# A hybrid attention and feed-forward block on one core: a double-buffered first stage, sums in smaller matmuls, an order by part, and one scaling moved from GpSimd to ScalarE

## The chip, the core and the metric

The kernel runs on one NeuronCore of one Trainium2 chip. The metric is the device time of one execution in microseconds (us). A core has five instruction streams that run side by side and meet only at semaphores: PE (TensorE, with its weight loads, PEld), DVE (VectorE), ACT (ScalarE), POOL (GpSimd) and SP (SyncE, which issues all DMAs here). Each stream executes in the order in which it is written, so an instruction that waits holds back all that stands behind it on its own engine.

## The reference, cut to what matters

The input is x of shape (4, 1024, 256): B = 4 sequences of L = 1024 rows. All is float32. Two blocks follow each other, each with a residual:

```python
def layernorm(x): return (x - mean(x)) / sqrt(var(x) + 1e-5)

h = layernorm(x)                                    # (4, 1024, 256), 4 heads of 64
q, k, v = silu(short_conv4(h @ W.T)) for Wq, Wk, Wv # causal, 4 taps per channel
beta = sigmoid(h @ Wb.T)                            # one per row and head
q, k = q * rsqrt(sum(q*q) + 1e-6), k * rsqrt(sum(k*k) + 1e-6)
# delta rule, per head, in chunks of 32 rows:
T = inverse(I + strictly_lower(beta * k @ k.T));  u = T @ (beta * v);  w = T @ (beta * k)
for chunk: u_adj = u - w @ S;  o = q @ S + lower(q @ k.T) @ u_adj;  S = S + k.T @ u_adj
local_s, local_m, local_l = depthwise causal FIR of v with 3, 15 and 63 taps
p = softmax((h @ gate_w + gate_b) / exp(log_temp)) * (1 - 5 eps) + eps   # 5 per head
o = p0*local_s + p1*local_m + p2*local_l + p3*delta + p4*v
x = x + layernorm(rmsnorm(o) @ Wo.T)

h = layernorm(x); hp = h shifted by one row
r = sigmoid(mix(h, hp, mu_r) @ Wr.T);  ka = relu(mix(h, hp, mu_k) @ Wk.T) ** 2
x = x + layernorm(r * (ka @ Wv.T))
```

## The kernel before, in words

The kernel cuts each sequence into 16 chunks of 64 rows and has five parts in time. Every engine has its own program, a list of small functions in an order written out by hand.

**First stage** (functions `a_...`, per sequence b = 0 to 3, `def sequence(b)` on each engine). DVE takes the statistics of 8 row tiles (L788, L792, L795), POOL the power -0.5 (L418), DVE normalizes (L802), PE transposes (L1142), ACT copies to `xnT` (L575), PE projects to v (L1152, four quarters q), ACT starts the convolution (L581), DVE adds its three other taps (L813), ACT applies silu (L587), PE transposes windows of v (L1163), and ACT copies each of them twice over, to `vwin` (L592) and to `vb` (L601, in two halves of 64 partitions), which SP stores in `v_scratch` (L272). The gates are 16 small matmuls of 24 columns per sequence (L1170), copied by DVE (L824). The input `xa`, the transposed rows `xnT` and the values `vb` have one buffer each: `a_xT_out` of a sequence waits for the matmuls and the stores of the one ahead of it, and `a_silu` for its last windows (`a_win`).

**FIR stage.** 64 tiles: matmuls against Toeplitz matrices that SP loads in 8 groups (`load(g)`, L255, L256), the gates' product on DVE (L892), two sums on POOL (L430, L432), transposes (L1222), and a copy to `fir`.

**Lead.** Chunks m = 0 to 7 are projected, convolved and silu'd to k and q (PE `proj` L1272, ACT `tap` L658, DVE `conv` L915, ACT `silu` L667), squared (L673) and summed (PE `sumsq` L1282, DVE `sumsq_out` L921, PE `sums_twice` L1288, DVE `norms_in` L931), and multiplied to grams (PE `gram` L1307, DVE `at_parts` L939, ACT `gram_out` L682). k and q share the PSUM banks 0 and 1 with those sums. SP stores a gram of each chunk and, after four chunks, loads them as blocks (`blocks_in`, L338). POOL then solves the group of four chunks, column after column, for 31 columns (`solve_column`, L499, L501). SP stores the solution (`solved_store`, L342) and loads it for each chunk (`solved_in`, L356, L361).

**Chunk steps n = 0 to 7** do chunk n of the scan and of all that follows, and the lead's work of chunk n + 8; groups 1 and 2 are solved meanwhile by POOL. **Steps n = 8 to 15**, the tail, have no lead work; group 3 is solved in the first of them. In each step run: the state's part (`scan_k` L1339, `rest_in` L975, `scan_u` L1348, `u_out` L697, `scan_o`), the mixed output (`o_scaled` L981, `o_summed` L987, `o_meansq` L991, L993, a power on POOL, `o_normed` L998), its projection (`o_turn` L1380, `y_rows`), three normalizations (`row_stats` L1005, L1009, L1012, a power on POOL (L510), `row_norm` L1017), and the feed-forward part (`shifted`, `mix` L1055, `ffn_k`, `ffn_r`, `ffn_v`, `ffn_out` L1064). POOL also makes the norms (L450, L453), scales the values by the keys' norm (`values`, L461), adds gated values and FIR parts (`direct`, L469, L472) and the last residual (`output`, L522). SP loads the values of chunk n (`values_in`, L304, L305) after `values` and `direct` of chunk n - 1.

All engines walk one table, `for n in range(-9, 19): chunk_step(n)`, in which lead, chunk and tail share one order.

## Time and profile before

| | |
|---|---|
| median of 3 runs | 829.26 us (817.76 to 842.99) |
| the profiled execution | 832.73 us, of which 830.9 us are the span |
| first stage, until the FIR stage's first matmul | 155.1 us |
| FIR stage, until the last transposes | 87.9 us |
| lead, until chunk 0's `rest_in` | 142.4 us |
| steps between `rest_in` of chunks 0 and 8 | 226.6 us |
| steps between `rest_in` of chunks 8 and 15 | 172.3 us |
| from `rest_in` of chunk 15 to the end | 46.7 us |

The times of the parts are cut at the start of an instruction of the trace: the first L1213 at 155.1, L975 of chunks 0, 4, 8, 12 and 15 at 385.4, 496.2, 612.0, 720.7 and 784.3 us. No engine is busy throughout: PE has 620.2 us of matmuls in the span (75%), DVE 494.2 (59%), POOL 424.8 (51%) and ACT 272.3 (33%).

### The profile page before, as it was taken

The page shows a single profiled execution, that of the slowest core. Times are in us where ns is not written, and L with a number is a line of the kernel's source. Part 1 is how long each engine was busy: PE and PEld are TensorE (multiplying, and loading weights), DVE is VectorE, ACT ScalarE, POOL GpSimd, SP SyncE. Part 2 cuts the span into 40 slices and gives each one's busy share as a digit, 9 for nine tenths or more (in the row PEclk, how much of TensorE's full clock was granted, in tenths as well). Part 3 has the DMA queues.
Part 4 walks back from the last instruction along what each step waited for, and adds up shares of the span by engine and source line. Part 5 has one row for each costly group of instructions (what it writes and reads, how often), then busy time and mean ns, then how long its engine had stood idle before and what let it go on. Part 6 is the DMA issues. An engine that isn't in the chain of part 4 may idle for free.

```text
span 830.9 us, 19290 instructions
## 1 busy us (share of the span) xinstructions
PE 620.2 (75%) x7556; PEld 496.5 (60%) x7556; DVE 494.2 (59%) x1194; ACT 272.3 (33%) x603; POOL 424.8 (51%) x513
## 2 busy tenths in 40 slices
PE   1866857488887774868878998988968576777854
PEld 1655646354555562657767886776767565666642
DVE  2556355343434433454688887878966575777762
ACT  1656564410114321333333344324412121222221
POOL 6000000155550000884889856998649998555521
PEclk9878777698988766698999998999998899999996
DMA  8723521288821114114212143321232020322101
GB/s 264 213 52 102 150 54 51 51 228 229 227 60 27 27 27 51 27 39 106 55 28 63 50 102 52 76 49 38 77 77 47 14 49 31 92 46 49 28 20 25
DMA packets 102634, 63.38 MB, mean 76 GB/s; under 512 B 81041, under 2 KB 95249, under 8 KB 100881
## 3 DMA queue, kind: packets, MB, share of 16 engines
q1 hardware_dynamic: 102544, 62.16, 29.2%
q8 instruction: 60, 0.98, 0.5%
q14 instruction: 30, 0.24, 0.1%
HBM read 43.19 MB, written 18.95 MB: 75 GB/s over the span
## 4 chain that ended last, share of the span: by engine, by line
POOL 39%; issue 13%; PE 7%; DVE 4%; SPq 3%; DMA 2%; ACT 1%; POOLq 0%; DVEq 0%; ACTq 0%
POOL seq L501 10%; POOL seq L499 8%; POOL arena L510 6%; POOL arena L450 4%; POOL arena L472 3%; PE bank L1272 3%; POOL arena L469 2%; SPq L338 2%; POOL arena L522 2%; POOL arena L461 2%; DVE arena L915 2%; PE bank L1282 1%; DMA seq<-gram_scratch 1%; PE bank L1307 1%; SPq L317 1%
## 5 line engine op out<-in xcount | busy, mean ns | idle before, releaser
L915 DVE SCALAR_TENSOR_TENSOR arena<-bank,small,arena 128x256 f32<-128x256 f32 x192 | 91.9, 482 | 40.6 <-ACT arena L658 35.9
L510 POOL TENSOR_TENSOR arena<-arena,neg_half 128x2 f32<-128x2 f32 (+1 forms) x64 | 64.3, 1005 | 91.0 <-DVE arena L1012 66.6
L501 POOL TENSOR_TENSOR seq<-seq 128x31 f32<-128x31 f32 (+15 forms) x124 | 85.4, 688 | 9.7
L499 POOL TENSOR_TENSOR seq<-seq 128x31 f32<-128x31 f32 (+15 forms) x124 | 70.2, 566 | 7.8
L1213 PE MATMUL bank<-arena 128*64 128x192 f32 x512 | 61.3, 367 | 11.5 <-DMA arena<-fms 7.1
L813 DVE SCALAR_TENSOR_TENSOR cva<-bank,small,cva 128x256 f32<-128x256 f32 x96 | 39.8, 477 | 50.3 <-ACT cva L581 50.1
L430 POOL TENSOR_TENSOR seq<-seq 128x256 f32<-128x256 f32 x32 | 23.3, 728 | 83.8 <-DVE seq L892 56.5
L892 DVE TENSOR_TENSOR seq<-bank,seq 128x384 f32<-128x384 f32 x64 | 35.3, 557 | 51.8 <-PE bank L1213 41.0
L658 ACT ACTIVATE arena<-bank,small 128x256 f32<-128x256 f32 x64 | 30.4, 475 | 75.5 <-PE bank L1272 75.5
L1152 PE MATMUL bank<-seq,w_v 128*128 128x259 f32 x128 | 45.2, 513 | 12.2 <-DVE cva L813 10.2
L1307 PE MATMUL bank<-arena 64*64 64x128 f32 x512 | 40.4, 303 | 17.8 <-issue 17.8
L418 POOL TENSOR_TENSOR rs_a<-ve_a,neg_half 128x8 f32<-128x8 f32 x4 | 6.6, 1642 | 92.1 <-DVE ve_a L795 92.1
L1272 PE MATMUL bank<-arena,w_k 128*128 128x268 f32 x128 | 46.3, 509 | 4.7 <-DVE seq L931 4.7
L1412 PE MATMUL bank<-seq,w_fk 128*128 128x256 f32 x128 | 34.9, 419 | 19.2 <-DVE seq L1055 19.2
L1213 PEld LDWEIGHTS bank<-arena 128*64 128x64 f32 x512 | 34.5, 148 | 23.5 <-DMA arena<-fms 7.7
L1272 PE MATMUL bank<-arena,w_q 128*128 128x268 f32 x128 | 36.7, 414 | 14.3 <-DVE arena L915 14.3
L481 POOL MEMSET seq<- 128x1024 f32 x4 | 3.8, 952 | 85.0 <-DVE seq L954 85.0
L450 POOL TENSOR_TENSOR arena<-seq,powers 128x16 f32<-128x16 f32 x16 | 46.4, 2902 | 0.3 <-POOL seq L501 0.3
L1307 PEld LDWEIGHTS bank<-arena 64*64 64x64 f32 x512 | 32.4, 151 | 21.3 <-issue 20.6
L1282 PEld LDWEIGHTS bank<-cst,arena 128*64 128x64 f32 x512 | 36.9, 158 | 12.3 <-issue 12.3
L1282 PE MATMUL bank<-cst,arena 128*64 128x32 f32 x512 | 38.4, 239 | 7.8 <-ACT arena L673 7.8
L1152 PEld LDWEIGHTS bank<-seq,w_v 128*128 128x128 f32 x128 | 31.5, 258 | 21.3 <-ACT seq L575 8.9
(137 smaller groups left out, 1499.6 us busy)
## 6 DMA issues: line engine op xcount, KB each, us to landing
arena<-fms SPq DMA_DIRECT2D x8, 1280.0 KB, 10.7
arena<-fl SPq DMA_DIRECT2D x8, 1024.0 KB, 5.3
arena<-xnT_scratch SPq DMA_DIRECT2D x32, 134.0 KB, 2.6
xnT_scratch<-seq SPq DMA_DIRECT2D x4, 1027.0 KB, 6.1
seq<-x SPq DMA_DIRECT2D x4, 1024.0 KB, 7.7
v_scratch<-seq SPq DMA_DIRECT2D x8, 512.0 KB, 5.3
arena<-v_scratch SPq DMA_DIRECT2D x16, 256.0 KB, 2.7
arena<-x SPq DMA_DIRECT2D x64, 64.0 KB, 2.3
```

What stands on the lines that cost most here:

```text
L450: pool.tensor_tensor(rk, ssel[:, slot_of(n)], powers[:, :, :], ALU.pow).then_inc(s["norms"], 1)
L499: pool.tensor_tensor(part, below, above, ALU.mult).then_inc(s["solve"], 1)
L501: last = pool.tensor_tensor(into, into, part, ALU.add)
L510: pool.tensor_tensor(dst, src, half8 if k == U else neg_half[:, 0:k], ALU.pow).then_inc(s[dst_sem], 1)
L813: nc.vector.scalar_tensor_tensor(cva[:, i, :], bank[2 + i][:, j:j + 256], conv_w[:, 2, i, j:j + 1], cva[:, i, :], ALU.mult, ALU.add).then_ ...
L892: nc.vector.tensor_tensor(fprod[:, q % (2 * FPAIRS), :], bank[q % 4][:, 0:2 * ROW], fgate[:, q // (TILES // 2), :], ALU.mult).then_inc(s[" ...
L915: nc.vector.scalar_tensor_tensor(cv[:, t], ps[:, :, j:j + C], conv_w[:, 1 - t // 2, t % 2, j:j + 1], cv[:, t], ALU.mult, ALU.add).then_inc ...
L1152: last = mm(bank[2 + oh][:, 0:PAD + 256], w["v"][:, kh, P * oh:P * oh + P], xnT[:, kh, 256 * q:256 * q + 256 + PAD], start=(kh == 0), stop ...
L1213: last = mm(out_[HH[i], :, 64 * hh:64 * hh + C], vwin[:, P * pr + 64 * hh + d, :], toep[:, g % 2, :, cin, :], start=True, stop=True)
L1272: last = mm(bank[g][:, 0:B * (C + PAD)], w["kq"[kind]][:, kh, P * g:P * g + P], xwin4[:, m % 2, kh], start=(kh == 0), stop=(kh == 1))
L1282: last = mm(bank[1][0:C, 32 * a:32 * a + 32], sq[:, a], headsel, start=True, stop=True)
L1307: last = mm(bank[2][q, P * u:P * u + P], kq5[q, slot_of(m), G4 * g + u, 0, :], kq5[q, slot_of(m), G4 * g + u], start=True, stop=True)
```

## The change

- **First stage.** `xa`, `xnT` and `vb` get a second set, carved from `fir`, which is free then. A sequence's input comes in two halves, each with its own semaphore. Statistics, powers and normalization go by halves and quarters. The small inputs and the v weights have semaphores of their own and stand ahead of the other weights. All engines' work of sequence b + 1 stands among that of sequence b.
- **Copies of v.** The values are stored with 128 columns of a pair of heads in a row; the two copies of 64 partitions per window become one of 128.
- **Gates.** 16 matmuls with the rows as weights become 8 with `w_gate` (padded to 32 columns) as weights and 256 rows moving, written to four groups of 32 PSUM partitions, then a copy on ACT and two transposes.
- **Sums of squares.** 16 matmuls (128 rows, 64 columns, 32 moving), a DVE step, one matmul and two DVE copies become 32 matmuls of 64 by 64 with 4 moving columns, k apart from q, and one DVE step.
- **FIR.** Its transposes come in pairs.
- **Order by part.** Every step is `lead_step(n)`, `chunk_step(n)`, `tail_step(n)` with an order of its own, and other offsets between the engines.
- **Keys' scale.** `values` moves from one POOL instruction to eight on ACT, one for each unit (sequence and pair).

```diff
-        xa = carve(seq, sa, M_TILES, D)
+        sx = [0]
+        xa2 = [carve(seq, sa, M_TILES, D), carve(fir_flat, sx, M_TILES, D)]
...
-        xnT = carve(seq, sa, HALVES, LP)
+        xnT2 = [carve(seq, sa, HALVES, LP), carve(fir_flat, sx, HALVES, LP)]
...
-        vb = carve(seq, sa, N, PAIRS, DK)
+        vb2 = [carve(seq, sa, N // 2, PAIRS, P), carve(fir_flat, sx, N // 2, PAIRS, P)]
...
             def values_in(n):
                 sp.wait_ge(s["vp"], n)
                 sp.wait_ge(s["ov"], 2 * n)
-                sp.dma_start(v_c, v_dram[n]).then_inc(s["v_in"], 16)
+                for hh in range(2):
+                    sp.dma_start(v_c[HH[hh]], v_dram[n][:, :, :, HH[hh]].rearrange("t r b d -> t (r b) d")).then_inc(s["v_in"], 16)
...
+            def values(n):
+                act.wait_ge(s["v_in"], 32 * n + 32)
+                act.wait_ge(s["norms"], 2 * n + 1)
+                act.wait_ge(s["rest"], n)
+                for u in range(U):
+                    last = act.activation(vp[:, u, :], v_c[:, u, :], ACT.Copy, scale=rk[:, 0, u:u + 1])
+                last.then_inc(s["vp"], 1)
...
-                if q == 0:
-                    act.wait_ge(s["a_proj"], b * 8)
-                    act.wait_ge(s["a_gate"], b * 1)
-                    act.wait_ge(s["a_xT_stored"], b * 16)
+                if q == 0 and b >= 2:
+                    act.wait_ge(s["a_proj"], (b - 1) * 8)
+                    act.wait_ge(s["a_gate"], b - 1)
+                    act.wait_ge(s["xT_odd_stored" if b % 2 else "xT_even_stored"], 16 * (b // 2))
...
-                for m in range(M_TILES):
-                    for kh in range(HALVES):
-                        last = mm(bank[6][:, H * NG * m:H * NG * (m + 1)], xnT[:, kh, PAD + P * m:PAD + P * m + P],
-                                  w_gate[:, kh, :], start=(kh == 0), stop=(kh == 1))
+                for kh in range(HALVES):
+                    for j in range(4):
+                        last = mm(bank[6][32 * j:32 * j + 32, 0:2 * P], w_gate[:, kh, :],
+                                  xnT2[b % 2][:, kh, PAD + 256 * j:PAD + 256 * j + 256], start=(kh == 0), stop=(kh == 1))
...
-                for a in range(2 * U):
-                    last = mm(bank[1][0:C, 32 * a:32 * a + 32], sq[:, a], headsel, start=True, stop=True)
-                last.then_inc(s["sumsq"], 1)
+                for u in range(U):
+                    for q in HH:
+                        last = mm(bank[1][q, NONE * (U * kind + u):NONE * (U * kind + u) + NONE], sq[q, U * kind + u], ones[q],
+                                  start=True, stop=True)
+                last.then_inc(s["sumsq_" + "kq"[kind]], 1)
...
-            for n in range(-9, 19):
+            for n in range(-10, 20):
+                lead_step(n)
                 chunk_step(n)
+                tail_step(n)
```

The order moves on all engines. Three places are shown: DVE in the first stage, SP where a group's solution is stored, and POOL in a step in which it solves.

DVE, first stage, in the middle of a sequence. L788 is the statistics, L792 and L795 their end, L802 the normalization, L813 the convolution (6 for a quarter), L824 the gates. Before:

```order
L813 SCALAR_TENSOR_TENSOR cva<-bank,small,cva 128x256 x18
L788 BN_STATS stats_a<-seq 128x6 x8
L792 BN_AGGR mv_a<-stats_a 128x2 x8
L795 TENSOR_SCALAR ve_a<-mv_a 128x8
L824 COPY gates<-bank 64x6x8 x8
L813 SCALAR_TENSOR_TENSOR cva<-bank,small,cva 128x256 x6
L802 TENSOR_SCALAR seq<-seq,mv_a,rs_a 128x256 x8
```

The change (L997 is the convolution, L985 the normalization, L1009 the gates, L970 the statistics):

```order
L970 BN_STATS stats_a<-fir 128x6 x4
L974 BN_AGGR mv_a<-stats_a 128x2 x4
L977 TENSOR_SCALAR ve_a<-mv_a 128x4
L997 SCALAR_TENSOR_TENSOR cva<-bank,small,cva 128x256 x6
L985 TENSOR_SCALAR seq<-fir,mv_a,rs_a 128x256 x2
L1009 COPY gates<-bank 64x6x8 x8
L997 SCALAR_TENSOR_TENSOR cva<-bank,small,cva 128x256 x6
L985 TENSOR_SCALAR seq<-fir,mv_a,rs_a 128x256 x6
```

The last normalization of a sequence stood at the sequence's end; it now stands two quarters earlier and in pieces between convolutions of the sequence ahead, so that its transposes can start while that one still runs.

SP, where the solution of group 1 is stored (`solved_scratch<-seq`). `arena<-v_scratch` is the load of a chunk's values, `arena<-xnT_scratch` of a window. Before:

```order
L323 DMA gram_scratch<-arena 128x512 [waits g_tok_1,g_tok_0]
L342 DMA solved_scratch<-seq 128x1024 [waits solved]
L305 DMA arena<-v_scratch 128x512 [waits ov,vp]
L317 DMA out<-arena 64x256 [waits y_out]
L317 DMA out<-arena 64x256 x3
L356 DMA seq<-gram_scratch 32x8x32 [waits off_a,turned,y_stored]
L361 DMA seq<-solved_scratch 32x8x32 x2
```

The change:

```order
L356 DMA solved_scratch<-seq 128x1024 [waits solved]
L370 DMA seq<-gram_scratch 32x8x32 [waits off_a,turned,y_stored]
L375 DMA seq<-solved_scratch 32x8x32 x2
L370 DMA seq<-gram_scratch 32x8x32
L375 DMA seq<-solved_scratch 32x8x32 x2
L312 DMA arena<-xnT_scratch 128x4x67 [waits proj_q0,proj_q1,proj_k1,proj_k0]
L312 DMA arena<-xnT_scratch 128x4x67
L319 DMA arena<-v_scratch 64x8x64 [waits ov,vp]
```

The load of the values stood right behind the store of the solution; it now also has the six loads of the solution (which wait until the store has landed) and two of a window ahead of it.

POOL, around the norms of chunk 2, while group 1 is solved (L499 and L501, in the change L536 and L538, are a column's product and sum; the powers of 128x8 belong to `o_normed`, those of 128x2 to the three normalizations). Before:

```order
L510 TENSOR_TENSOR arena<-arena,neg_half 128x2 [waits st2]
L450 TENSOR_TENSOR arena<-seq,powers 128x16 [waits vp,norms,ssel]
L453 TENSOR_TENSOR arena<-gates,arena 128x8 [waits o1,norms]
L461 TENSOR_TENSOR arena<-arena 128x512 [waits rest,norms,v_in]
L499 TENSOR_TENSOR seq<-seq 128x11x21 [waits solve]
L501 TENSOR_TENSOR seq<-seq 128x11x21 [waits solve]
L499 TENSOR_TENSOR seq<-seq 128x12x20 [waits solve]
L501 TENSOR_TENSOR seq<-seq 128x12x20 [waits solve]
L499 TENSOR_TENSOR seq<-seq 128x13x19 [waits solve]
L501 TENSOR_TENSOR seq<-seq 128x13x19 [waits solve]
L510 TENSOR_TENSOR arena<-arena,neg_half 128x8 [waits oms]
L469 TENSOR_TENSOR arena<-arena,gates 128x512 [waits o2,v_in]
```

The change:

```order
L547 TENSOR_TENSOR arena<-arena,neg_half 128x8 [waits oms]
L553 COPY arena<-arena 128x8 [waits xf,mix_r,mix_k]
L495 TENSOR_TENSOR arena<-seq,powers 128x16 [waits vp,norms,ssel]
L498 TENSOR_TENSOR arena<-gates,arena 128x8 [waits o1,norms]
L506 TENSOR_TENSOR arena<-arena,gates 128x512 [waits o2,v_in]
L509 TENSOR_TENSOR arena<-arena,fir 128x512 [waits ov]
L547 TENSOR_TENSOR arena<-arena,neg_half 128x2 [waits st1]
L536 TENSOR_TENSOR seq<-seq 128x11x21 [waits solve]
```

The scaling (L461) is gone from POOL, and no column is left between the norms and `direct` (L506, L509): the columns of a step now all stand between the power that waits for `st1` and the one that waits for `oms`.

## Rows read from the trace of the kernel before

**Rows 1.** Busy time by engine in nine stretches (us from the span's start).
```profile
core 0: us, PE busy (x) PEld busy (x) DVE busy (x) ACT busy (x) POOL busy (x), PEclk, DMA share, GB/s
20.00:155.10 135.10, 92.33 (x442) 76.13 (x440) 72.17 (x226) 81.72 (x180) 4.92 (x3) 0.76 0.32 96
155.10:243.00 87.90, 76.03 (x603) 45.42 (x604) 35.32 (x64) 10.26 (x19) 46.53 (x64) 0.90 0.65 179
249.00:315.00 66.00, 50.37 (x329) 38.59 (x327) 28.52 (x68) 23.07 (x57) 0.00 (x0) 0.73 0.10 26
496.20:612.00 115.80, 103.10 (x1631) 86.72 (x1630) 94.42 (x220) 43.15 (x100) 90.12 (x109) 0.97 0.27 62
612.00:720.70 108.70, 74.89 (x1302) 64.79 (x1302) 68.22 (x152) 23.03 (x44) 90.45 (x109) 0.89 0.21 48
720.70:784.30 63.60, 50.24 (x980) 43.37 (x980) 47.46 (x112) 17.27 (x33) 38.02 (x34) 1.00 0.20 45
```
**Rows 2.** Groups by line, first stage: busy us, mean ns, idle before, releaser.
```profile
L813 DVE SCALAR_TENSOR_TENSOR cva<-bank,small,cva 128x256 f32<-128x256 f32 x96 | 39.8, 477 | 50.3 <-ACT cva L581 50.1
L601 ACT ACTIVATE seq<-bank 64x256 f32<-64x256 f32 x64 | 24.4, 381 | 1.6
L1170 PE MATMUL bank<-w_gate,seq 128*128 128x24 f32 x128 | 18.0, 297 | 0.0
L788 DVE BATCH_NORM_STATS2 stats_a<-seq 128x6 f32<-128x256 f32 x32 | 10.9, 414 | 17.0 <-DMA small<-smalls 11.9 <-DMA seq<-x 5.1
```
**Rows 3.** Timeline: projection quarters 0 and 1 of sequence 0.
```profile
20.10 2.92 PE L1152 MATMUL bank<-seq,w_v 128*128 128x259 f32 x8
25.38 1.99 PE L1152 MATMUL bank<-seq,w_v 128*128 128x259 f32 x8 [1.92 <-DVE cva L813]
```
**Rows 4.** Timeline of the FIR stage: 8 matmuls.
```profile
159.43 1.48 PE L1213 MATMUL bank<-arena 128*64 128x192 f32 x16
```
**Rows 5.** Timeline of the lead: chunks 2 and 3.
```profile
281.07 3.88 PE L1272 MATMUL bank<-arena,w_k 128*128 128x268 f32 x8 [0.67 <-DVE seq L931]
291.47 3.47 PE L1282 MATMUL bank<-cst,arena 128*64 128x32 f32 x32 [0.91 <-ACT arena L673]
294.87 1.97 PE L1307 MATMUL bank<-arena 64*64 64x128 f32 x16
298.07 3.91 PE L1272 MATMUL bank<-arena,w_k 128*128 128x268 f32 x8 [0.67 <-DVE seq L931]
```
**Rows 6.** Timeline: store and load of group 0's solution, next values.
```profile
374.60 0.33 SPq L342 DMA_DIRECT2D solved_scratch<-seq  x1
377.22 0.66 SPq L356 DMA_DIRECT2D seq<-gram_scratch  x1
383.10 0.38 SPq L305 DMA_DIRECT2D arena<-v_scratch  x1
```
**Rows 7.** Groups by line, chunk steps.
```profile
L461 POOL TENSOR_TENSOR arena<-arena 128x512 f32<-128x512 f32 x16 | 18.1, 1132 | 0.0
L1282 PE MATMUL bank<-cst,arena 128*64 128x32 f32 x512 | 38.4, 239 | 7.8 <-ACT arena L673 7.8
L1329 PE MATMUL bank<-seq 32*32 32x32 f32 x512 | 11.5, 195 | 0.0
L645 ACT ACTIVATE seq<-bank 64x128 f32<-64x128 f32 x2 | 0.4, 264 | 6.0 <-PE bank L1237 6.0
```
**Rows 8.** DMA issues: KB each, us to landing.
```profile
arena<-v_scratch SPq DMA_DIRECT2D x16, 256.0 KB, 2.7
```
**Rows 9.** Windows with L501 alone: its busy time in two solves.
```profile
331.00:374.60 43.60, 20.80 (x31) 0.83 0.12 32
496.20:612.00 115.80, 21.52 (x31) 0.97 0.27 62
```
**Rows 10.** Timeline: `o_summed` beside a busy POOL and beside a quieter one.
```profile
568.41 1.48 DVE L987 TENSOR_TENSOR arena<-arena 128x512 f32<-128x512 f32 x1
748.03 0.69 DVE L987 TENSOR_TENSOR arena<-arena 128x512 f32<-128x512 f32 x1
```

869 lines of the change are left out of this document (577 added, 292 removed).

## The prediction

> **What bounds the kernel now.** The first view is the table of stretches [rows 1], because the change touches parts with different limits. From 20 to 155.1 us, the first stage, no engine is full: PE is busy for 92.3 of 135.1 us, ACT for 81.7, DVE for 72.2. In the groups by line [rows 2] DVE's convolution waits 50.1 us for ACT's first tap, and nothing but one quarter of one sequence is under way: a latency bound. In the FIR stage PE is busy for 76.0 of 87.9 us. The lead (249 to 315) is a chain too, with PE busy for 50.4 of 66 us. From 496.2 to 612.0, four chunk steps, PE is busy for 103.1 of 115.8 us, DVE for 94.4, POOL for 90.1: near a bound of three engines. In the tail POOL is full while it solves a group (90.5 of 108.7), and after that (720.7 to 784.3, three steps of 21.2) nobody is: PE 50.2, DVE 47.5, POOL 38.0 of 63.6 us.
>
> **The first stage.** Work per sequence, from [rows 1, 2]. DVE: 72.2/4 = 18.0 us. ACT: 81.7/4 = 20.4, less half of L601 (24.4/2/4 = 3.1), plus one copy of a gate bank (0.4) = 17.7. PE: 92.3/4 = 23.1 at a mean granted clock of 0.76, less the gates' 18.0/4 = 4.5, plus the new gates. Those are 8 matmuls over 256 columns. Four matmuls of the projection over 259 columns take 1.99 us [rows 3], so one after another the new gates take 4.0. In the FIR stage 8 matmuls of 192 columns, alternating between two groups of 64 columns, take 1.48 us [rows 4], 0.96 ns per column against 1.92, so two groups run side by side. I take that factor of two, 2.0 us, and 0.3 for the two transposes: PE 20.9.
> The Trainium skill, "TensorEngine Tiling (Array Packing)", section Key Properties, lets different tiles run in parallel; with four tiles it would be 1.0 us and the stage 4 us shorter in all. The same section says that a change of the tiling mode drains the engine, which speaks against gates of 32 columns between matmuls of 128; no row shows a gap of a size that matters.
> Now a sequence takes (155.1 - 20.1)/4 = 33.8 us. With two sets of buffers b + 1 can fill the waits of b, and the limit is PE's 20.9. Three engines in a fixed order with quarter steps don't fit without loss: I take 22.5. The ends: 18.0 (DVE's sum, PE at a better clock) and 28 (half of the waits stay). Start: DVE's first statistics wait until 11.9 for the small inputs, the last of the first DMAs [rows 2]; half a sequence ahead of the weights frees about 7.5 us, so that quarter 1 of sequence 0 is projected at 20 rather than 27.4 [rows 3]. Then 3 x 22.5 = 67.5, and for the rest of the last sequence 20.5 (three quarters of a sequence and 4 us of the softmax's start, which now stands ahead of the last convolution). FIR starts at 108, against 155.1: **-47** (-61 to -27). The values' stores move 512 instead of 256 bytes in a piece; what waits for them at the stage's end waits as before.
> **FIR stage.** Same loads, same products, transposes in pairs: 0 (-3 to +3).
>
> **The lead.** One chunk takes 298.07 - 281.07 = 17.0 us [rows 5]. The chain: projections of k at 281.07 until the last square of q, which frees L1282 at 291.47 (10.4, unchanged), sums 3.47, second gram 1.97, one more matmul and DVE's two copies until 298.07. In the change the k sums run earlier, and of the q sums there are 16 small matmuls. The nearest row is L1329, 16 matmuls in 32x32 at 11.5/16 = 0.7 us [rows 7]; the other end is half of the old sums, 1.7. I take 1.0. The gram follows, and DVE's one step runs beside it. 10.4 + 0.3 (the square of the other half is now last) + 1.0 + 1.6 (the gram at a mixed clock) = 13.3. Four chunks: 4 x 3.7 = 14.8, less 1.4 because the fourth gram is read out after, no longer ahead of, the next projection, and 1 because the first chunk was shorter: **-12** (-16 to -5). The solve of group 0 and the transfers around it stay: they wait for that gram.
>
> **Steps 0 to 7.** PE loses per step 38.4/16 = 2.4 plus 0.4 and gains 1.4 for the sums: about 1.4 less, 24.4. DVE 23.3, POOL per step without the scaling (1.13 [rows 7]) 21.4 on average, but unevenly: a solve is 62 instructions, 39 us, plus a gap of 0.08 after each, 44 us in three steps, the middle one the heaviest (columns of 256 elements). Beside it POOL has 11.5 us a step. So the three steps cost POOL 12, 17, 11.5 of columns + 11.5 + 1.5 of waits for DVE = 25, 30, 24.5; in the lighter two DVE (23.3 + 2.5 of waits for powers) sets 26. The fourth is PE's or DVE's, 25.2. That is 107.2 for a group, against 115.8.
> A new wait takes part of it back. SP now has the load of chunk 4's values behind the solution's store, six loads and two more. From store to the same place took 383.10 - 374.60 = 8.5 us, and the values take 2.7 more [rows 6, 8], 11.2 in all. POOL's last column ends 3.6 us ahead of step 3's start (0.3, the wait for `o_meansq`, 1.9 for the power, and idle time), so the values land at 7.6, while `direct` wants them at 3.5. POOL loses 4.1, of which 2.8 reach DVE's `residual` by way of `f_normed`. So 110 for a group. Steps 4 to 7: 110 against 115.8. Steps 0 to 3: 26 + 30 + 26 + 28, against 110.8 with a first step of 24.9: no gain. **-5** (-16, when the wait is hidden, to +6).
> ACT's eight scalings replace one instruction of 1.13 us. Nearest is L645, 0.26 us for 128 columns [rows 7]: 2.1 us for the eight, beside other work, as ACT is busy for 43 of 115.8 us.
>
> **The tail.** Steps 8 to 10 are POOL's: 25, 30, 24.5, step 11 about 20.5, together 100, against 108.7; I take -6. Steps 12 to 15, walked in the new order: DVE's 15.8 us, plus its waits for three powers (3), for `direct`, which now stands behind the second power (0.8), and for PE and ACT ahead of `shifted` (0.6) = 20.2, against 21.2: -3. After chunk 15 `ffn_out` of older chunks is out of the way: -2. **-11** (-18 to +4).
>
> **Sum.** -47 - 12 - 5 - 11 = -75: 832.7 - 75 = 757.7 for a profiled execution. The one shown lies 0.4% above the median of the runs, so 755 on the median's scale.
>
> **Rivals.**
> *A, the orders fit better.* The transfers hide and steps 0 to 7 come to PE's 25.2 on average: 8 x (28.3 - 25.2) = 25, 20 more than above: 735. For it speaks that such an order is possible by the sums; against it the middle third on POOL.
> *B, the first stage stays a chain.* With a period of 28 FIR starts at 20 + 84 + 24 = 128: 775. For it: the clock of 0.76, at which PE alone needs 21, and three engines that hand each other pieces of half a microsecond.
> *C, POOL and DVE hold each other up.* `o_summed` took 1.48 us beside POOL's scaling and 0.69 elsewhere [rows 10], while L501's 31 sums took 20.8 us beside an idle DVE and 21.5 beside a full one [rows 9], so that POOL hardly suffers. If in a denser step the columns slow down by 10% and DVE's five two-input steps by a third, 9 solve steps get 2 us each: 773. The Trainium skill, "GPSIMD Engine Reference", Specifications, says that the SBUF interfaces are shared with VectorE and contended by instructions with two SBUF inputs; by this rule it is C.
> *D, slower.* SP's queue gates every step: `values_in` waits for ACT's scaling and POOL's `direct` with the output, gram and x transfers queued behind it, and if each of 14 further steps waits as long as the whole chain of 6.5 us beyond the need, 14 x 6.5 = 91: 846, which is where 2% slower begins. Against it: SP's list for a step is about 15 us of issues in 26.
> *E, no gain that counts:* B and half of D together, 816 to 848.
>
> **Numbers.** Forecast 0.55, A 0.12, B 0.17, C 0.10, D 0.03, E 0.03. Two per cent is about what a measurement of this kernel tells from no change (its own runs lie within 1.6% of the median), so below 813 is faster. Faster 0.94, same 0.03, slower 0.03. The range takes in A, B and C with the first stage's own ends: 733 to 790.
>
> **What would show it.** The first FIR matmul at 108 (100 to 118), with PE over 85% busy between 25 and 100. The k projections of the lead 13.3 apart. The load of values at SP's head 8 us after the second solution's store, POOL idle for about 4 us ahead of chunk 4's `direct`, and steps of 26, 30, 26 and 28 us. L461's successor on ACT at 0.2 to 0.3 us each. Tail steps of 20.2. It is wrong if the first stage ends after 125, or if the steps that solve stay at 30.

## The result, and the profile after

The changed kernel takes 786.2 us in the median of four runs (785.3 to 789.75), against 826.15 us for the kernel before (817.76 to 842.99, four runs of the same comparison). The ratio is 0.956, with a 95% interval of 0.947 to 0.965. The forecast was 755 us with a range of 733 to 790: the sign held, and the range did with 4 us to spare, but the gain in the profiled spans is 47.4 us (830.9 to 783.5), where 75 were forecast. Cut at the same instructions as before (the first FIR matmul, the lead's first projection, `rest_in` of chunks 0, 4, 8, 12 and 15):

| part | before | after | change | forecast |
|---|---|---|---|---|
| first stage | 155.2 | 114.2 | -41.0 | -47 |
| FIR stage | 93.7 | 89.8 | -3.9 | 0 |
| lead | 136.5 | 125.8 | -10.7 | -12 |
| steps 0 to 3 | 110.8 | 113.6 | +2.8 | 0 |
| steps 4 to 7 | 115.8 | 118.7 | +2.9 | -5.8 |
| steps 8 to 11 | 108.7 | 108.2 | -0.5 | -6 |
| steps 12 to 14 | 63.6 | 68.8 | +5.2 | -3 |
| end | 46.6 | 44.5 | -2.1 | -2 |

Of the 27.6 us that are missing, 24 lie in the steps and the end, 6 in the first stage and 1 in the lead; the FIR stage gave back 4. Each part is one trace, and how far a part moves by itself can be read from the runs below. In the changed kernel and the nine of them that leave both parts' programs as they are (e1 to e8 and x3, apart from a few loads), the FIR stage takes 85.0 to 94.0 us and the lead 119.4 to 128.5. So the 3.9 us of the FIR stage are within that spread, and the 10.7 of the lead are not. The busy times of the changed kernel by stretch, in the columns of [rows 1]:

```profile
20.00:114.20 94.20, 58.33 (x370) 45.48 (x370) 67.76 (x213) 62.83 (x148) 5.03 (x5) 0.86 0.52 151
443.36:562.07 118.71, 104.48 (x1784) 88.32 (x1783) 96.41 (x222) 50.69 (x133) 86.56 (x105) 0.96 0.29 62
562.07:670.23 108.16, 76.94 (x1281) 65.68 (x1282) 63.46 (x141) 29.29 (x75) 80.68 (x100) 0.79 0.21 46
670.23:739.00 68.77, 58.24 (x973) 48.78 (x973) 48.09 (x113) 22.57 (x57) 33.42 (x30) 0.88 0.21 46
```

POOL's work fell in steps 8 to 11 from 90.5 to 80.7 us (4.9 of that are the four scalings, most of the rest is work that now falls outside the stretch), yet they take as long. In the last stretch the granted clock fell from 1.00 to 0.88, and PE's busy time rose from 50.2 to 58.2 us; DVE's is nearly the same (47.5 and 48.1).

**First stage.** From the timeline, PE's first quarters of sequences 1 and 2 with DVE's wait; the window from 31 to 52 us in the columns of [rows 1]; SP's issues; then the group by line of DVE's convolution, and transfers of the window from 36 to 75 us with their time to landing:

```profile
33.83 1.99 PE L1396 MATMUL bank<-fir,w_v 128*128 128x259 f32 x8 [1.11 <-DVE cva L997]
51.48 1.99 PE L1396 MATMUL bank<-seq,w_v 128*128 128x259 f32 x8 [1.11 <-DVE cva L997]
70.94 1.41 DVE L970 BATCH_NORM_STATS2 stats_a<-fir 128x6 f32<-128x256 f32 x4 [19.22 <-DMA fir<-x]
```
```profile
31.00:52.00 21.00, 17.00 (x115) 13.64 (x115) 20.35 (x66) 18.02 (x45) 2.01 (x2) 1.00 0.53 142
```
```profile
42.51 1.13 SPq L270 DMA_DIRECT2D arena<-fl  x1
43.68 1.12 SPq L271 DMA_DIRECT2D arena<-fms  x1
...
47.55 1.41 SPq L254 DMA_DIRECT2D fir<-x  x2
```
```profile
L997 DVE SCALAR_TENSOR_TENSOR cva<-bank,small,cva 128x256 f32<-128x256 f32 x96 | 40.1, 478 | 7.3 <-ACT cva L653 7.0
```
```profile
arena<-fms SPq DMA_DIRECT2D x2, 1280.0 KB, 18.0
...
fir<-x SPq DMA_DIRECT2D x2, 512.0 KB, 23.7
```

The same quarter of the next sequence comes 17.6 us later (51.48 - 33.83), a pace well below the 22.5 of the forecast: DVE no longer waits 50 us for the first tap [rows 2] but 7. Then DVE stands for 19.2 us. The rows of the last sequence are asked for at 47.55 behind the FIR stage's first taps, four transfers of 4.6 MB together, and a store of 1 MB, and take 23.7 us to land. The forecast's sum of a slower pace and no such wait came out near the truth for the wrong reason. The Trainium skill, "DMA: Bandwidth & Descriptors", section on queues, rings and completion order, says that descriptors of a ring are consumed in order; the trace fits this, since the same pair of transfers for the sequence ahead, asked for at 22.2 with no taps in front, landed in 7.5 us by the same view. It doesn't tell the order in the ring from plain sharing, as the DMA engines were busy throughout (a share of 1.01 from 48 to 55 us, at 231 GB/s).

**The lead.** The projections of k stand 12.2 us apart, where 17.0 was before [rows 5] and 13.3 forecast. Timeline, the projections of k of two chunks:

```profile
216.07 3.21 PE L1540 MATMUL bank<-arena,w_k 128*128 128x268 f32 x8
...
228.23 3.56 PE L1540 MATMUL bank<-arena,w_k 128*128 128x268 f32 x8
```

**Step 3**, where group 1's solution is handed over. The timeline, with the store (L356), the normed output (L1188), the load of chunk 4's values (L319), the solved blocks' first product (L1583), the turn of the output (L1645) and POOL's direct part (L506):

```profile
424.40 0.34 SPq L356 DMA_DIRECT2D solved_scratch<-seq  x1
426.19 0.69 DVE L1188 TENSOR_TENSOR arena<-arena 128x512 f32<-128x512 f32 x1 [0.53 <-POOL arena L547]
431.73 1.23 SPq L319 DMA_DIRECT2D arena<-v_scratch  x2
432.00 1.06 PE L1583 MATMUL bank<-seq 32*32 32x32 f32 x32 [4.74 <-DMA seq<-solved_scratch]
432.99 1.97 PE L1645 MATMUL bank<-cst,arena 64*64 64x64 f32 x32
435.41 1.06 POOL L506 TENSOR_TENSOR arena<-arena,gates 128x512 f32<-128x512 f32 x1 [5.50 <-DMA arena<-v_scratch]
```

The predicted wait is there: the load of the values comes 7.3 us behind the store (8.5 in the forecast), and POOL stands for 5.5 us. A second one was not predicted. PE has the solved blocks' product ahead of `o_turn` (L1645), so the output, normed at 426.9, is turned only at 433.

**The tail**, step 13. POOL's direct part (L506, L509), DVE's `x_normed` (L1207), the next load of values, PE's first solved product and `y_rows` (L1652):

```profile
698.68 1.06 POOL L506 TENSOR_TENSOR arena<-arena,gates 128x512 f32<-128x512 f32 x1
698.74 2.73 DVE L1207 TENSOR_SCALAR arena<-seq,arena 128x256 f32<-128x256 f32 x2 [0.81 <-POOL arena L547]
699.81 1.51 POOL L509 TENSOR_TENSOR arena<-arena,fir 128x512 f32<-128x512 f32 x1
701.40 1.23 SPq L319 DMA_DIRECT2D arena<-v_scratch  x2
707.69 0.71 DVE L1150 STREAM_TRANSPOSE seq<-seq 128x512 f32<-128x512 f32 x1 [1.48 <-DMA seq<-solved_scratch]
711.21 3.78 PE L1652 MATMUL bank<-w_o,arena 128*128 128x256 f32 x8
```

And the groups by line for two of the three forms of L1207 (x from SBUF, y from PSUM) and for ACT's values:

```profile
L1207 DVE TENSOR_SCALAR arena<-seq,arena 128x256 f32<-128x256 f32 x32 | 30.3, 988 | 16.0 <-POOL arena L547 16.0
L1207 DVE TENSOR_SCALAR arena<-bank,arena 128x256 f32<-128x256 f32 x32 | 15.9, 539 | 11.2 <-POOL arena L547 11.1
L841 ACT ACTIVATE arena<-arena 128x64 f32<-128x64 f32 x128 | 32.2, 336 | 7.8 <-POOL arena L495 3.9 <-DMA arena<-v_scratch 3.9
```

Two instructions of `x_normed` take 2.73 us beside the direct part, and 0.73 in the last chunk's step, which has none; the mean of one was 408 ns before and is 988 now. `y_rows` takes 3.78 us here and 1.99 in step 11: from 710 to 716 us the granted clock is 0.50. SP's next loads, of values and behind them of solved blocks, wait for the same direct part and land late: DVE waits 1.48 us here and 6.2 in the three steps.

### The profile page after: what moved, and what is told of

It reads as the page before. It is cut to its first block, busy times and chain, and to the rows that moved or that the text cites. A ratio compares the mean times of both kernels' runs of the same rounds, so it can differ in the third digit from the quotient of the medians.

```text
span 783.5 us, 20240 instructions
## 1 busy us (share of the span) xinstructions
PE 592.6 (76%) x7980; PEld 477.9 (61%) x7980; DVE 492.6 (63%) x1166; ACT 284.2 (36%) x703; POOL 407.5 (52%) x502
## 4 chain that ended last, share of the span: by engine, by line
POOL 30%; PE 14%; issue 10%; DVE 8%; SPq 7%; DMA 3%; ACT 1%; POOLq 0%; DVEq 0%; ACTq 0%
POOL seq L538 10%; POOL seq L536 9%; POOL arena L547 4%; PE bank L1652 4%; PE bank L1540 2%; POOL arena L509 2%; POOL arena L495 2%; DVE arena L1112 2%; SPq L352 2%; SPq L375 2%; PE bank L1572 2%; PE bank L1551 1%; POOL arena L506 1%; PE bank L1645 1%; DMA seq<-gram_scratch 1%
## 5 line engine op out<-in xcount | busy, mean ns | idle before, releaser
L547 POOL TENSOR_TENSOR arena<-arena,neg_half 128x2 f32<-128x2 f32 (+1 forms) x64 | 61.9, 966 | 110.4 <-DVE arena L1202 74.4
L1112 DVE SCALAR_TENSOR_TENSOR arena<-bank,small,arena 128x256 f32<-128x256 f32 x192 | 91.7, 482 | 38.2 <-ACT arena L775 33.6
L538 POOL TENSOR_TENSOR seq<-seq 128x31 f32<-128x31 f32 (+15 forms) x124 | 86.7, 699 | 9.7
L536 POOL TENSOR_TENSOR seq<-seq 128x31 f32<-128x31 f32 (+15 forms) x124 | 71.6, 577 | 8.3
L1479 PE MATMUL bank<-arena 128*64 128x192 f32 x512 | 57.0, 372 | 13.2 <-DMA arena<-fms 10.7
L1479 PEld LDWEIGHTS bank<-arena 128*64 128x64 f32 x512 | 38.5, 155 | 25.5 <-DMA arena<-fms 11.4
L1572 PEld LDWEIGHTS bank<-arena 64*64 64x64 f32 x512 | 34.1, 157 | 27.3 <-issue 26.9
L495 POOL TENSOR_TENSOR arena<-seq,powers 128x16 f32<-128x16 f32 x16 | 49.6, 3101 | 0.3 <-POOL seq L538 0.3
L997 DVE SCALAR_TENSOR_TENSOR cva<-bank,small,cva 128x256 f32<-128x256 f32 x96 | 40.1, 478 | 7.3 <-ACT cva L653 7.0
L1540 PE MATMUL bank<-arena,w_q 128*128 128x268 f32 x128 | 36.0, 404 | 10.7 <-DVE arena L1112 10.7
L775 ACT ACTIVATE arena<-bank,small 128x256 f32<-128x256 f32 x64 | 29.4, 471 | 40.5 <-PE bank L1540 40.5
L1652 PE MATMUL bank<-w_r,seq 128*128 128x256 f32 x128 | 35.1, 421 | 9.6 <-DVE seq L1245 9.6
L784 ACT ACTIVATE arena<-arena 128x256 f32<-128x256 f32 x64 | 25.7, 413 | 40.6 <-DVE arena L1112 40.3
L1207 DVE TENSOR_SCALAR arena<-seq,arena 128x256 f32<-128x256 f32 x32 | 30.3, 988 | 16.0 <-POOL arena L547 16.0
L1652 PE MATMUL bank<-w_o,arena 128*128 128x256 f32 x128 | 38.1, 449 | 1.4 <-ACT arena L827 1.4
L462 POOL TENSOR_TENSOR rs_a<-ve_a,neg_half 128x4 f32<-128x4 f32 x8 | 8.2, 1028 | 58.8 <-DVE ve_a L977 58.6
## 6 DMA issues: line engine op xcount, KB each, us to landing
arena<-fms SPq DMA_DIRECT2D x8, 1280.0 KB, 12.2
```

The lines of the kernel that those rows point to most:

```text
L495: pool.tensor_tensor(rk, ssel[:, slot_of(n)], powers[:, :, :], ALU.pow).then_inc(s["norms"], 1)
L536: pool.tensor_tensor(part, below, above, ALU.mult).then_inc(s["solve"], 1)
L538: last = pool.tensor_tensor(into, into, part, ALU.add)
L547: pool.tensor_tensor(dst, src, half8 if k == U else neg_half[:, 0:k], ALU.pow).then_inc(s[dst_sem], 1)
L997: nc.vector.scalar_tensor_tensor(cva[:, i, :], bank[2 + i][:, j:j + 256], conv_w[:, 2, i, j:j + 1], cva[:, i, :], ALU.mult, ALU.add).then_ ...
L1112: nc.vector.scalar_tensor_tensor(cv[:, t], ps[:, :, j:j + C], conv_w[:, 1 - t // 2, t % 2, j:j + 1], cv[:, t], ALU.mult, ALU.add).then_inc ...
```

## Experiments

Times are medians of four runs or more, ratios are to the kernel before on the same chip (0.956 for the changed kernel). As these medians move by 1% between executions, what one stretch takes is read from the traces, from `rest_in` to `rest_in`. That is one trace for each kernel, and two kernels with the same steps 0 to 7 (e3 and e7) differ there by 1.8 us in sum.

### Steps 3 and 7: one wait, the other, and both

The values first, on SP (e1):
```diff
+ if 1 <= n + 4 < 9: values_in(n + 4)
  if 0 <= n + 2 < 8 and solving(n + 2)[1] == 2: solved_store(...)
  ...
- if 1 <= n + 4 < 9: values_in(n + 4)
```


> Of steps 0 to 7, on SP's queue, the load of a chunk's values is moved ahead of the wait for the solved group (the changed kernel has it behind: at 431.73 us, after the store at 424.40). Theory V (the values' load behind the solved store is what makes steps 3 and 7 long): the load of chunk 4 is issued before 424, POOL's direct no longer waits 5.5 us for it and runs at about 430, step 3 (30.0) and the two steps at group 2 (34.1 and 29.4) lose 3 to 5 us each time: 775 to 780 against 786. Theory T (the solved blocks' own load, for which TensorE's order stands 4.7 us until 432.0, is the bound): TensorE starts off_first at 432.0 all the same, nothing or at most 1 us per group is gained: 784 to 787.

The solved blocks later on three engines in steps 3 and 7 (e2):
```diff
  PE : - off_first(n + 1); o_turn(n); gram(n + 8, 0); y_rows(n); off_second(n + 1); gram(n + 8, 1)
       + o_turn(n); gram(n + 8, 0); y_rows(n); off_first(n + 1); gram(n + 8, 1); off_second(n + 1)
  ACT: off_out(n + 1) behind oT_out(n) and gram_out
  DVE: solved_turn(n + 1), at_parts(n + 8, 1) and residual(n) behind y_stats(n), ahead of off_in(n + 1)
```


> In steps 3 and 7 alone, TensorE does off_first of the next chunk behind y_rows and not ahead of o_turn; ACT's off_out goes behind oT_out and VectorE's block transpose behind the statistics of y, so that the normed output, its turn and the product with the output weights no longer stand behind the load of the solved blocks. SP's order is the changed kernel's. Theory T: the output turn starts at about 427 in place of 433, so 4 us go at step 3 and as many at step 7: 777 to 780. Theory V: chunk 4's values still land at 435, POOL's direct and ACT's scaled values with them, and the residual of the next chunk waits for these: 784 to 787.

Both (e3 = e1 + e2):

> Both edits together: values' load ahead of the solved store, and TensorE, ACT and VectorE past the solved blocks in steps 3 and 7. If the two waits stand side by side and either alone keeps the step long (each of the single edits gives little), this gives 8 to 11 us: 775 to 778. If one alone is the bound, it equals that one. A rival (C of the prediction, the two engines hold each other up): the stall only gives way to slower vector work and a POOL that is late with the next group's solve, and the gain is under 3 us.

Measured: e1 782.6 us (0.937, 0.927 to 0.946), e2 788.8 us (775 to 790, and one run of 1049 us whose cause is unknown; they scatter too much for a ratio), e3 775.6 us (0.928, 0.920 to 0.935). By the traces step 3 took 30.6 us in the changed kernel, 29.8 in e1, 33.6 in e2 and 28.1 in e3; step 7 took 34.1, 34.2, 37.7 and 30.8. Both single-cause theories fall: in e1 POOL's direct part ran at 428.0 without a wait, but PE still stood 4.6 us; in e2 the output was turned at 426.7, but POOL and ACT stood for the values until 435. The waits stand side by side, and only both edits remove them. Why e2 makes both steps 3 us longer than they were wasn't looked into. The 8 to 11 us expected of e3 came in the median (10.6 under the changed kernel), but not in the steps: from chunk 0 to 15 its trace takes 405.2 us against 409.2. The timeline of e3: the store, the turn, POOL's direct part, the solved product, and then the last gram of the group, read out by ACT (L799), stored (L337) and loaded back (L352):

```profile
418.66 0.34 SPq L356 DMA_DIRECT2D solved_scratch<-seq  x1
421.44 1.15 PE L1652 MATMUL bank<-cst,arena 64*64 64x64 f32 x32
424.13 1.06 POOL L506 TENSOR_TENSOR arena<-arena,gates 128x512 f32<-128x512 f32 x1
426.10 0.69 PE L1590 MATMUL bank<-seq 32*32 32x32 f32 x32
430.39 0.38 ACT L799 ACTIVATE arena<-bank 128x256 f32<-128x256 f32 x1
...
441.37 0.53 SPq L337 DMA_DIRECT2D gram_scratch<-arena  x1
...
445.41 9.11 SPq L352 DMA_DIRECT2D seq<-gram_scratch  x16
```

Yet the four steps from chunk 3's `rest_in` to chunk 7's take 115.2 us in the changed kernel, 115.4 in e1, 114.9 in e4 and 115.2 in e3 (113.2 in e7 below, with the steps of e3, and 120.3 in e2). From the store of group 1's solution until POOL begins on group 2 pass 43.5 us in the changed kernel and 43.5 in e3, and from there to the next store 71.7 in both. Another bound holds there: the last gram of a group is read out at 430.8, waits in SP's queue until 441.4, and comes back by 16 loads, 9.1 us of issues; DVE scales it at 459.0, and POOL, idle for 10.1 us in one piece meanwhile, begins to solve at 462 and has columns until the next handover. The old order was better here. POOL's first instruction of group 2's solve, in the kernel before and in the changed one:

```profile
510.65 0.95 POOL L481 MEMSET seq<- 128x1024 f32 x1
```
```profile
467.87 0.95 POOL L518 MEMSET seq<- 128x1024 f32 x1
```

That is 14.5 us behind chunk 4's `rest_in` before (496.2) and 24.5 in the changed kernel (443.4). For group 3 it is 13.8 and 21.7 us behind chunk 8's.

### The tail: POOL's neighbour

```diff
  def tail_step(n):   # POOL
+     if 9 <= n < N: direct(n)
      if 7 <= n - 3 < N: output(n - 3)
      power(n - 1, "st1", ...); solve_part(n - 1, 2); power(n - 1, "st2", ...)
-     if 9 <= n < N: direct(n)
```


> In the last eight steps POOL does the direct part (L506, L509) of a chunk at the start of its step, ahead of the output add of an earlier chunk, and no longer between the power for x and the norms, where VectorE's x_normed (L1207) ran beside it in 2.73 us for two (0.73 in the kernel before). Theory N (neighbour: POOL's two-input sums slow the vector engine, and the wait for them holds back SP's loads of the values and of the solved blocks): L1207 back to 0.73 for two in these steps, the values' load 7 to 10 us earlier, VectorE's 1.5 to 2.3 us wait for the solved blocks gone: 2.0 + 0.6 to 1.3 us for each of 7 steps, steps 12 to 15 20.2 to 21 us each, 763 to 772 against 786. Rival K (clock): the steps are 22 to 23 long since TensorE's clock is lower than in the kernel before (0.85 against 1.00), the matmul y_rows took 3.78 us for eight where 1.9 is full speed, and that stays: at most 4 us of gain, 782 or more. Rival M (moved): the slowing goes to f_normed and off_in, beside which the direct part now stands, and from them to the statistics of y: half the gain, 775 to 780.

Measured: 769.6 us (0.928, 0.920 to 0.936). Timeline of e4's tail, the direct part and the two SBUF forms of L1207; the window of e4's step 13, in the columns of [rows 1]; then the same step in the changed kernel; then in e1, whose tail has the changed kernel's order, with its `x_normed`:

```profile
709.51 1.06 POOL L506 TENSOR_TENSOR arena<-arena,gates 128x512 f32<-128x512 f32 x1
709.57 2.74 DVE L1207 TENSOR_SCALAR arena<-arena 128x256 f32<-128x256 f32 x2 [0.81 <-POOL arena L547]
...
718.42 0.73 DVE L1207 TENSOR_SCALAR arena<-seq,arena 128x256 f32<-128x256 f32 x2 [0.81 <-POOL arena L547]
```
```profile
694.91:713.74 18.83, 16.90 (x325) 14.40 (x324) 15.97 (x39) 7.40 (x19) 10.97 (x10) 1.00 0.25 54
```
```profile
694.05:716.94 22.89, 19.86 (x325) 16.57 (x326) 16.10 (x38) 7.52 (x19) 11.73 (x11) 0.85 0.21 45
```
```profile
692.80:712.87 20.07, 16.91 (x325) 14.37 (x325) 16.04 (x38) 7.52 (x19) 11.15 (x10) 1.00 0.19 41
697.49 2.74 DVE L1207 TENSOR_SCALAR arena<-seq,arena 128x256 f32<-128x256 f32 x2 [0.81 <-POOL arena L547]
```

The last steps fall from 23.8, 22.9 and 22.0 us to 19.2, 18.8 and 18.8, under the 20.2 of the forecast. `x_normed` is back at 0.73, the slowing moved to `f_normed` (2.74), and DVE's waits for the solved blocks fell from 6.2 us in three steps to 0.4.

But most of the gain is the clock. It is 1.00 again, the level of 2.4 GHz, and `y_rows` takes 1.99. In e1 step 13 ran at 1.00 too, with `x_normed` as slow as in the changed kernel and the same order, and took 20.1 us against 22.9 at 0.85. So of the 4.1 us that this step lost in e4, the clock accounts for 2.8, and the neighbour and the earlier loads together for 1.2. Rival K had the larger cost right; its claim that the low clock stays is false. Without the edit (the changed kernel, e1 to e3, x2 and x3 below) three of eighteen such steps ran at 1.00; with it (e4 to e8) all fifteen did, at 18.8 to 19.8 us. That the shorter waits keep the clock up is argued from this count and not shown: up to 15 us into step 13 the changed kernel and e1 agree within 0.1 us, and then one has the low clock and the other not.

The 769.6 us lie in the range of theory N, but by a sum that it didn't have, since steps 8 to 11 got 10 us longer (118.2 against 108.2). Steps 8 (33.1, 29.5 before the edit) and 11 (28.5, 23.4) became longer: while POOL solves, a direct part ahead of the power for y is on the chain. So it was done from chunk 12 on alone, with both edits of steps 3 and 7 (e7, `if 12 <= n < N: direct(n)` ahead of `output`):

> The kernel with both edits of steps 0 to 7, and the direct part ahead of the output add from chunk 12 on alone; steps 8 to 11 keep the changed kernel's order (in the kernel that moved the direct part everywhere they took 118 us in place of 108). Theory N (neighbour and SP's loads behind the direct part): the three steps 12 to 14 take 18.8 to 19.5 us each in place of 22 to 24, the end 42 to 43: 10 to 13 us under the kernel with both edits, 763 to 767. Rival: step 11 gets what the later steps lose (28.5 in place of 23.4, as it did where the direct part was moved everywhere, since POOL stands for chunk 12's values ahead of the power for y): 768 to 773.

Measured: 765.8 us (0.924, 0.918 to 0.930), step 11 at 23.7, steps 12 to 14 at 18.9, 18.8 and 18.8.

### The loop from the last gram to the solution

The two edits of e3 and three more at once (e5), in part wrong:
```diff
  SP  : + blocks_in(g, first three chunks) one step earlier, behind rows_out;  blocks_in(g, last chunk) in its place
  DVE : blocks_scaled(g) right behind o_normed(n)
  POOL: + norms_power(n + 1) ahead of the power for o;  + 5 columns at the end of steps 0 and 4, in step 8 ahead of norms_q
  POOL: + if 12 <= n < N: direct(n) ahead of output;  SP: values_in(12) ahead of the last solved_store
```


> The two edits of steps 0 to 7 together, and three more. (1) Blocks early: of a group's 16 block loads SP issues the 12 of its first three chunks a step earlier, so that only four stand between the last gram's store and the solve (16 took 9 us of SP's queue, 445.4 to 454.5 us in the kernel with both edits); VectorE scales the blocks right behind o_normed. (2) Solve early: in steps 0, 4 and 8 POOL takes the power for the norms into its idle time ahead of the power for o (it waited 8 to 10 us there) and begins the next group's solve with 5 columns in that step; the columns are shared out anew. (3) Tail: the values of chunk 12 are loaded ahead of the last solved store, and the direct part stands ahead of the output add from chunk 12 on (18.8 us a step there in the kernel with direct moved away). Theory L (steps 4 to 7 take 115.2 us in every kernel so far, since the loop last gram, store, 16 loads, scaling, POOL's 31 columns, solved store, next chunk closes on itself): the loop is shortened by 4 to 7 us, steps 4 to 7 take 105 to 111; with steps 8 to 11 some 3 to 8 shorter and 12 to 15 at 18.8 to 19.5: 745 to 757. Rival P (TensorE is the bound there, busy 101 to 104 of the 115 us): steps 4 to 7 stay at 112 or more, only the tail gains: 760 to 768.

Measured: 774.1 us (0.933, 0.925 to 0.941), no better than e3. Steps 5 and 6 fell to 27.8 and 27.5, but step 4 took 39.1 and step 8 34.0. One row of the waits from 442 to 482 us, for step 4:

```profile
DVE seq L1178 <- DMA seq<-gram_scratch: 7.6, 1, 7.6
```

The last gram still stood behind SP's other work until 454.0, and DVE, which now had the scaling ahead of its other work, stood 7.6 us for it. A wait had been moved onto the chain. So SP's order was written anew (e6), and POOL's columns trimmed (e8):

```diff
  SP, n in (0, 4):
+   gram_store(n+9); rows_in(n+2); values_in(n+4); rows_out(n); rows_in(n+3); gram_store(n+10)
+   solved_store(g); solved_in(n+4); blocks_in(g+1, first three); window_in(n+12); values_in(n+5)
+   gram_store(n+11); blocks_in(g+1, last)
  SP, n == 8: + solved_in(12) right behind solved_store;  POOL: group 3's last columns one place earlier
```


> The trace of the kernel with all five edits showed why its first step of a group took 39.1 us: the last gram of the group was ready at about 431 us but stood in SP's queue until 454, behind output stores and loads, and VectorE stood 7.6 us for the blocks. Here SP's order around steps 0 and 4 is written anew: rows and the third gram ahead of the solved store, then the solved blocks of the next chunk, the 12 early block loads, the values, the last gram and its four loads, and only then the rest; VectorE scales the blocks in the step before (behind the first convolution of the next chunk), POOL begins groups 2 and 3 with 5 and 4 columns ahead of the power for o and gives the last group's solve fewer columns in step 11; in step 8 the solved blocks are asked for right behind the store. The tail has the direct part ahead of the output add from chunk 12 on. Theory L (the loop from the last gram to the solved store bounds steps 4 to 8, and SP's queue order is most of its slack): steps 4 to 7 take 106 to 111 us, steps 8 to 11 96 to 104, steps 12 to 14 18.8 each: 742 to 758. Rival P (TensorE's 101 to 104 busy us and VectorE's 94 of 115, with POOL's 86, leave no room): steps 4 to 7 at 113 or more, total 762 to 772.

```diff
- DVE n in (3, 7): conv(n + 9, 0); blocks_scaled     + n == 3: blocks_scaled; conv(12, 0);  group 3: in step 8
- POOL n == 4: 5 columns ahead of the power for o, 2 behind output;  n == 0: 5
+ POOL n == 4: 5 columns ahead of the power for o;                   n == 0: 3
```


> The kernel with the new SP order around the groups (758.5 us), with POOL's early columns put where they delay nothing: in its trace the 5 columns ahead of the power for o held that power back by 3.1 us and the two behind the output add held the power for y back by 2.9 us, in step 4 (33.7 us), and VectorE's scaling stood behind a convolution that waited for ACT. Here group 2 begins with 5 columns ahead of the power for o and none behind, its blocks are scaled ahead of that convolution, group 1 begins with 3 in place of 5, and group 3's blocks are scaled behind the residual of step 8. Theory L: step 4 takes 27 to 29 us, step 7 29 to 31, the rest as it was: 747 to 753. Rival P (the columns only move, and steps 5 to 7 take back what step 4 gives): 755 to 760.

Measured: e6 758.5 us (0.915, 0.908 to 0.922), e8 759.4 us (0.916, 0.909 to 0.922). These two are the fastest, some 3.5% below the changed kernel by the medians (4% by the ratios), and can't be told apart; e7, measured beside e6, has 765.8. (The ratios of e6 and e7 rest on a kernel before that scattered from 818 to 849 us beside them.) In e6 the last gram was stored 23.8 us behind chunk 3's `rest_in`, in place of 34.3 in e3. Window of steps 4 to 7 of e8 (a trace of its fastest run, 749.7 us):

```profile
430.90:544.70 113.80, 105.60 (x1816) 89.10 (x1812) 96.79 (x222) 50.73 (x133) 87.42 (x105) 0.97 0.30 64
```

Steps 4 to 7 take 118.7 us in the changed kernel, 118.4 in e6 and 113.8 in e8, steps 8 to 11 108.2, 101.7 and 104.2. From chunk 3 to chunk 7 the 115.2 us (113.2 in e7) became 110.7 and 112.1. In e8 POOL begins on group 2 only 25.6 us behind the store, in place of 43.5, but the solve then takes 85.2 us in place of 71.7. The loop was a bound, then, but shortening it gave 1 to 4.5 us there, less than theory L's 106 to 111 for steps 4 to 7: in e8 PE is busy for 105.6 of 113.8 us and its first three steps take 28.5, 28.0 and 27.6, which fits PE as the next bound and was not tested. In steps 8 to 11, where PE has slack, the earlier solve did pay, by 4 to 6.5 us against the changed kernel and 8 to 10 against e7 (112.1). In e8 steps 4 and 7 took what its own theory L gave them (28.5 and 29.7), yet the median is that of its rival: steps 5 and 6 took 4.3 us more than in e6, and steps 8 to 11 2.5.

### What the parts and the order are worth

The order by part undone, in the changed kernel:
```diff
- for n in range(-10, 20): lead_step(n); chunk_step(n); tail_step(n)
+ for n in range(-9, 19): chunk_step(n)      # the order of the kernel before, on all five streams
+ ...; ktok_out(n + 1); values(n + 1)        # ACT
+ ...; sumsq(n + 8, 0); sumsq(n + 8, 1)      # PE
```


> The changed kernel with its order by part undone: SP, POOL, ACT, VectorE and TensorE run the steps in the order of the kernel before (one chunk_step for all), with the new sums, with the keys' scale of the values on ACT behind ktok_out, and with the new first stage. By the terms of the prediction (lead -12, steps -5, tail -11 by the order) this is 20 to 28 us above the changed kernel: 806 to 814. By what the trace of the changed kernel shows (lead 10.5 shorter, but the 16 steps 10 longer than before), the order is worth nothing in sum: 780 to 792, the lead longer by about 10 and the steps shorter by as much.

One part alone, in the kernel before:
```diff
  POOL: norms(n + 1)  - values(n + 1)
  ACT : off_out(n + 1); ktok_out(n + 1)  + values(n + 1)   # eight units
```


> The kernel before with one part of the change alone: the keys' scale of the values on ACT, eight units, behind ktok_out of the next chunk in ACT's order, and gone from POOL. Theory W (the eight units stand at the end of ACT's queue and VectorE's residual waits for them; in the kernel with the old order and all the new parts the residual waited 2.06 to 3.3 us for them in every step, and the tail steps took 23.9 to 24.2 in place of 21.2): the tail steps take 23.5 to 24.5, the first step of each group 5 to 10 more, 848 to 872 against 830. Theory Z (they are hidden as they were on POOL, and the lengthening there comes from the sums or from the values' two loads): 825 to 836.

Measured: the old order with the new parts 812.3 us (0.978, 0.969 to 0.987); the values on ACT alone in the kernel before 859.2 us, slower by 3.4% (1.034, 1.027 to 1.041). The row for the residual in the latter, by line, and DVE's wait for the units in the window from 671 to 743 us (steps 11 to 13) of the former:

```profile
L975 DVE TENSOR_TENSOR arena<-arena,bank 128x512 f32<-128x512 f32 x16 | 11.0, 687 | 31.6 <-ACT arena L715 29.1 <-issue 2.5
```
```profile
DVE arena L1045 <- ACT arena L777: 6.0, 3, 2.1
```

In that place of ACT's list the eight units of 2.0 us stand on the chain, and the residual waits 31.6 us, 29.1 of them for the units, where it waited 5.1 in the kernel before: that is the whole 26 us. (In its last steps the granted clock is 0.86 and they take 24.1 us, so a part of the loss may reach the time by way of the clock; the two aren't separated.) In the new order the units are early and the last steps have no such wait. So in a kernel with the moved scaling the order by part saves about 26 us by the medians (29 in the steps: 438.2 against 409.2 us from chunk 0 to 15). That is the 20 to 28 of the forecast's terms only by luck: they had the lead's 12 us in them, and the lead is as short in the old order (121.4 us) as in the new (125.8), so that its gain is the sums'. And the saving is about as large as the bill of the moved scaling in the old order, so without that scaling the order may be worth little; old order, new parts and the scaling on POOL were not run together.

The first stage in the old order, with both sets:
```diff
- for b in range(-1, 5): sequence(b)        # three engines: pieces of b and b + 1 in turn
+ for b in range(B): sequence(b)            # one sequence after the other; norm of b + 1 behind conv(b, 3)
```


> The changed kernel with its two buffer sets, its tile forms and its early loads in the first stage, but each engine goes through a sequence as before, one sequence after the other, and the next sequence's norm stands behind the last convolution. Theory O (the interleaved orders are what overlaps the sequences; the sets only allow them): the first stage is a chain of about 35 us per sequence again, less what the early loads and the single gate product save: first FIR matmul at 135 to 150 in place of 114, total 807 to 822. Theory S (the second set and the early loads do it, the order is a detail): first FIR matmul at 112 to 122, total 784 to 794.

Measured: 791.9 us (0.948, 0.938 to 0.957), not to be told from the changed kernel by the runs. In the trace the first FIR matmul is at 127.7, between the theories: 27.5 us of the 41 come with the sets, the early loads and the new tile forms, 13.5 with the order. Its first quarters stand 28.2, 27.8 and 26.2 us apart: the sets alone give rival B's period and its 128. DVE's wait for the tap, 50.1 in [rows 2], is 37.9 there and 7.0 in the changed kernel, which has the 19.2 us wait beside it.

The scaling back on POOL, in the new order:
```diff
  POOL: norms(n)  + values(n)  ... direct(n);   ACT: - values(n)
```


> The changed kernel with the keys' scale of the values back on POOL, one multiplication of 128x512 right behind the norms (1.06 us by the like one for the gate), in place of eight units on ACT (2.0 us for eight). Theory P (POOL is the bound in the steps in which it solves, 5 to 7, 1 to 3 and 9 to 11, and its work is on the chain): 1.1 us a step in some 9 to 12 steps, and POOL's two-input work beside VectorE a little more: 795 to 801. Theory A (the eight units on ACT end later than the one on POOL would, 2.0 against 1.1 us, and the residual waits for them): no change or a gain: 782 to 788.

Measured: 790.4 us (776 to 800, too scattered for a ratio). In the trace the steps from chunk 0 to 15 take 419.5 us against 409.2, the last three 68.8 in both: 10 us in the steps with a solve, as theory P says, but the whole execution shows 3 (its lead was 6 shorter, with the same program), so the size isn't settled.

## Why the prediction was half right

**First stage, -47 forecast, -41 found.** The mechanism holds, and so does the start (quarter 1 of sequence 0 at 20.6, 20 forecast); both sizes in the rest of the sum failed, in opposite directions: three periods are 15 us less and the wait is 19 more. The period is 17.6, not 22.5: DVE was busy for 20.35 of 21.0 us between 31 and 52, so three engines do fit in a fixed order, down to the fullest one's sum of 18.0 (the end that I had priced and not taken). But I looked at how long SP's issues take, not at what lies in the queue behind them, and missed the 19.2 us. Rival B, a period of 28, is false for the changed kernel. PE was busy for 47 of 75 us between 25 and 100, far from the 85% that I gave as the sign. Whether the stage would end at 95 without the wait (the taps asked for behind the last rows) was not tried and stays open.

**FIR stage and lead.** -3.9 for 0, within what this stage moves from trace to trace; -10.7 for -12, by the term that was costed (the 16 sums; k projections 12.2 apart for 13.3), with a spread of some 5 us either way.

**Steps 0 to 7, -5 forecast, +5.7 found.** The stall was right in place and near in price (2.8 us to the residual; 2.5 in step 3 by e3, which took out two waits), though PE's own wait stands beside it and either alone keeps the step long. What failed is "that is 107.2 for a group". I summed POOL's load for the steps that solve and let the fourth be PE's, as if the solve could start when that step starts. It starts 24.5 us later (467.9, against 443.4), when the blocks are back, and the 115 us of the changed kernel, e1, e3 and e4 fit that loop: gram, SP's queue, blocks, columns, store. So the steps that solve are 5, 6 and 7 (28.5, 29.9 and 34.1 us, for the forecast's 30, 26 and 28), and the stall falls on a full one. The kernel before had a start at 14.5 us: the new order made the loop's first arc longer, and I had no term for it. In [rows 1] three engines near full hid it. The sum has a slip too: the three parts of columns, 12, 17 and 11.5, make 40.5 us, where I had counted 44 for a solve. POOL's longest waits between 412.8 and 528 in the changed kernel (8.2, 5.5, 3.6 and 2.6 us) all lie ahead of that start.

**Tail, -11 forecast, +2.6 found.** In steps 8 to 11, -0.5 for -6, the solve of group 3 starts 21.7 us into step 8, where the kernel before had 13.8; with a start at 7.5 (e6) they take 101.7. In steps 12 to 14, +5.2 for -3, what failed is a term that isn't in the sum: I left the clock at the 1.00 of [rows 1], and it was 0.85, 0.86 and 0.92, worth 2.8 us in step 13. At a clock of 1.00 the step does take 20.1 us (e1), for 20.2 forecast, with DVE busy for 16.0, for 15.8; three such steps would be 3.3 us shorter than before. That this fits so well is luck in part, since the durations in it are from the old neighbourhood: `x_normed` cost 2.0 more a step beside the direct part, and DVE waited 2.1 for the late loads. Rival C had the mechanism, but I applied it to steps with two inputs alone, half of the rule in the Trainium skill, "GPSIMD Engine Reference", Specifications. `x_normed` has one tensor input; from SBUF it takes 0.37 us for 256 columns, from PSUM 0.50. The form from PSUM kept its 539 ns (538 before), the SBUF form went from 408 to 988. The page names DVE instructions with two SBUF inputs and those in a 2-port mode; the trace agrees, if the faster form is in that mode. The other side was missed too and sets that off: `o_normed`, 1721 ns before beside POOL's work, fell to 719.

**Parts and order.** I costed ACT's scaling at nothing, "beside other work". That is right in the new order and would have been 26 us wrong in the old one. A didn't happen: steps 0 to 7 take 29.0 us on average, for its 25.2. D and E didn't either; SP's queue does hold things up, not by its length in a step but by what stands ahead of four transfers a group. The 786.2 us lie inside the range, but at none of the values that the forecast or a rival had, and by a mixture of errors.

## What to carry to other kernels

Compare stretches at the same granted clock before giving a difference to an edit: in the last steps two traces with the same order there differ by 2.8 us in one step by the clock alone. An instruction's price belongs to its place: before moving one, list what will run beside it, on GpSimd for an instruction of VectorE and the other way round, and what stands behind its wait on every queue it passes. Where two waits on different engines end at the same event, remove both before judging either. And for a stage that several near-full engines share, look for the one idle stretch per period: here it marked a loop through memory that no sum of busy times shows.

## What the runs showed of the hardware

- One float32 instruction of DVE from SBUF to SBUF (128x256, one tensor input) takes 0.37 us, and two of them 2.73 us beside POOL's two-input product and sum of 128x512 (1.06 and 1.51 us). That is a factor of 3.7, where the forecast had taken a third. Beside columns of the solve it took 1.28 us for two (products and sums of 128x192) and 2.02 (128x252), while the form from PSUM kept 0.99 (128x231). Beside the 128x512 work the form from PSUM never stood.
- A sequence's new gates, eight matmuls over 256 columns in four column tiles of 32 (16 in the profile, which shows each float32 matmul twice), end within 1.07 us, half of the 2.0 that I took:

```profile
22.51 1.07 PE L1419 MATMUL bank<-seq,w_gate 128*32 128x256 f32 x16
```

  The rule weighed in the forecast, from the Trainium skill's "TensorEngine Tiling (Array Packing)", gave 1.0: the trace agrees.
- In the last steps the granted clock was 0.88 in the changed kernel and 1.00 in e4, with the same PE work in 22 to 23.8 and in 18.8 us steps, and 1.00 in one step of e1, with the changed kernel's order, in 20.1 us; `y_rows` took 3.78 us in the first and 1.99 in the second, near the factor of two between the levels of 1.2 and 2.4 GHz.
